# Four PSUM additions spread through the step of a graph attention, with a wait for each PSUM bank and a semaphore for the rescale

## The reference

```python
Q = (enh @ Wq + bq).reshape(N, H, D)
K = (enh @ Wk + bk).reshape(N, H, D)
V = (enh @ Wv + bv).reshape(N, H, D)
mod_k = K[src] + 0.2 * rel[:, None, :]
scores = jnp.einsum('ehd,ehd->eh', Q[dst], mod_k) / D ** 0.5
seg_max = jax.ops.segment_max(scores, dst, num_segments=N)
ex = jnp.exp(scores - seg_max[dst])
denom = jax.ops.segment_sum(ex, dst, num_segments=N)
w = ex / denom[dst]
agg = jax.ops.segment_sum(w[:, :, None] * V[src], dst, num_segments=N)
```

## Time and profile before

| | |
|---|---|
| median of 3 runs | 4579.15 us (4568.29 to 4586.91) |
| the profiled execution's own time | 4569.27 us |
| its span in the trace | 4567.5 us |
| busy over the span | PE 64%, DVE 57%, POOL 33%, ACT 26% |
| attention stage in the trace | first `modify` at 1051.1 us, last addition at 1880.2 us |
| DVE busy, in a stretch of 100 us of the middle of that stage | 84.8 to 89.1 us |
| PE busy, in the same | 69.5 to 75.1 us |

### The profile page before, as it was taken

The page is one execution under the profiler, slowest core; times in us unless marked ns, Lnnn a source line. Parts: engine busy times, 40 slices in busy tenths (PEclk is TensorE's granted clock), DMA queues, the critical chain, the costliest instruction groups (busy, mean ns, idle before and its releaser), DMA issues. The chain is left out here.

```text
span 4567.5 us, 54034 instructions
## 1 busy us (share of the span) xinstructions
PE 2922.7 (64%) x12877; PEld 1992.2 (44%) x12878; DVE 2614.3 (57%) x5653; ACT 1173.5 (26%) x4381; POOL 1510.3 (33%) x1422
## 2 busy tenths in 40 slices
PE   5555553254777777332095388988888628899980
PEld 4344442143444554122074244444444326677650
DVE  7766663346888888254812178788878830022221
ACT  0000000001555555201021044344444312233320
POOL 0377776005555554000000134344334305011114
PEclk9999999986778777565598689899889859999995
DMA  0000004315665665110000233333333307111112
GB/s 28 2 4 4 4 4 15 79 52 186 177 179 170 179 179 132 55 35 14 20 0 3 74 89 103 90 95 98 96 88 101 84 28 141 44 32 33 33 36 74
DMA packets 236997, 326.44 MB, mean 71 GB/s; under 512 B 115196, under 2 KB 166816, under 8 KB 236633
## 3 DMA queue, kind: packets, MB, share of 16 engines
q0 software_dynamic: 84512, 224.41, 19.0%
q1 hardware_dynamic: 117971, 95.44, 7.8%
q10 hardware_dynamic: 34402, 5.30, 1.0%
HBM read 291.54 MB, written 32.86 MB: 71 GB/s over the span
## 5 line engine op out<-in xcount | busy, mean ns | idle before, releaser
L1257 POOL DMA_INDIRECT g_rows<-h_d,g_idx x432 | 415.0, 961 | 1418.5 <-ACT g_idx L1272 1311.9
L925 POOL DMA_INDIRECT a_strip<-kv_d,src x416 | 433.5, 1042 | 593.3 <-POOLq L74 262.4
L484 POOL DMA_INDIRECT rec_d<-rec_s,place x400 | 476.2, 1190 | 243.9 <-issue 218.6
L949 ACT ACTIVATE x<-a_strip,x 128x64 f32<-128x64 f32 x1664 | 411.0, 339 | 223.9 <-PE a_psv L994 209.2
L994 PE MATMUL a_psv<-x 128*125 128x260 f32 x832 | 309.3, 507 | 157.8 <-DVE agg L1088 125.2
L384 PE MATMUL ps_base<-start,lo_hot_t 125*125 125x25 f32 x800 | 184.8, 384 | 264.0 <-DVE picked L439 263.3
L1350 PE MATMUL g_psa<-g_msg,g_hot 128*125 128x256 f32 x832 | 280.3, 468 | 110.3 <-DVE g_msg L1443 110.3
L384 PEld LDWEIGHTS ps_base<-start,lo_hot_t 125*125 125x125 f32 x800 | 175.5, 326 | 341.1 <-issue 339.6
L1338 PE MATMUL g_pso<-w_o,g_ut 128*128 128x256 f32 x840 | 294.0, 432 | 4.5 <-ACT g_lk L1280 4.5
L1350 PEld LDWEIGHTS g_psa<-g_msg,g_hot 128*125 128x125 f32 x832 | 161.8, 215 | 272.2 <-issue 169.6
L994 PEld LDWEIGHTS a_psv<-x 128*125 128x125 f32 x832 | 180.0, 240 | 222.6 <-DVE agg L1088 120.4
(11 more groups left out here) (374 smaller groups left out, 5722.1 us busy)
## 6 DMA issues: line engine op xcount, KB each, us to landing
a_row<-rows_d SPq DMA_DIRECT2D x104, 256.0 KB
e_w<-in_L_ffn_W1p SPq DMA_DIRECT2D x8, 1024.0 KB
e_w<-in_L_ffn_W2p SPq DMA_DIRECT2D x8, 1024.0 KB
y_d<-e_y SPq DMA_DIRECT2D x56, 128.0 KB, 1.7
g_rows<-h_d,g_idx POOLq DMA_INDIRECT x432
a_strip<-kv_d,src POOLq DMA_INDIRECT x416
rec_d<-rec_s,place POOLq DMA_INDIRECT x400
x<-in_x SPq DMA_DIRECT2D x2, 3125.0 KB
```

What stands on the lines that cost most here:

```text
L484: pool.indirect_dma_start(out=m.rec_d[:, :], out_offset=bass.IndirectOffsetOnAxis(ap=place[b][:, u:u + 1], axis=0), in_=rec_s[b][:, u, :], ...
L925: pool.indirect_dma_start(out=strip[:, lane.start + u, place:place + 2, :].rearrange("p a d -> p (a d)"), out_offset=None, in_=m.kv_d[:, : ...
L949: act.activation(msg[b][:, u, h, 0:HD], strip[:, lane.start + u, place, h * HD:(h + 1) * HD], ACT.Copy, scale=w[:, k * U + u, h:h + 1])
L1257: pool.indirect_dma_start(out=rows[r][:, u, 64:512], out_offset=None, in_=m.h_d[:, :], in_offset=bass.IndirectOffsetOnAxis(ap=idx[r][:, u: ...
```

## The change

It has four parts. The four additions, which stood in two pairs, are put one by one between the large DVE instructions: after `make`, after `modify`, after `multiply` and after `total`. `one_hot` moves from behind `total` to a place between the second addition and `multiply`. Each matmul of `aggregate` waits for the addition that last read its own bank, instead of both for all additions ahead. The rescale counts on a semaphore `s_scaled`, for which only DVE's next addition waits, and it moves with the register load to the head of the iteration.

```diff
         def added(s, u):
-            return 1 + s * U + u + s // CS
+            return 1 + s * U + u
...
                 if half == 0:
                     pe.wait_ge(s_hot, s + 1)
                     pe.wait_ge(s_wv, s + 1)
-                pe.wait_ge(s_add, added(s, 2 * half))
                 for u in (2 * half, 2 * half + 1):
+                    pe.wait_ge(s_add, added(s, u) - 1)
                     pe.matmul(ps_v[u % 2][:, 0:H * HW], hot[b][:, u, :],
...
+            def add(s, u, tiles):
+                if s < 0:
+                    return
+                dve.wait_ge(s_mm, s * U + u + 1)
+                dve.wait_ge(s_add, added(s, u))
+                if u == 0 and s >= CS and s % CS == 0:
+                    dve.wait_ge(s_scaled, s // CS)
+                agg = m.agg[:, tiles[u], :, :].rearrange("p h d -> p (h d)")
+                dve.tensor_tensor(agg, agg, ps_v[u % 2][:, 0:H * HW], ALU.add).then_inc(s_add, 1)
...
                 linked = 0 <= c < NC
+                tiles = node_tiles(v, ENGINE.DVE) if v >= 0 else None
+                if v > 0 and v % CS == 0:
+                    rescale(v // CS)
                 if now + 2 < STEPS:
                     make(now + 2)
                 if k == 0 and linked:
                     in_tile(c)
                 if k == 1 and linked:
                     raise_top(c)
+                add(v, 0, tiles)
                 if now < STEPS:
                     modify(now)
+                add(v, 1, tiles)
+                if 0 <= now - LAG < STEPS:
+                    one_hot(now - LAG)
+                if now < STEPS:
                     multiply(now)
-                if v >= 0 and v % CS == 0 and v:
-                    rescale(v // CS)
-                if v >= 0:
-                    tiles = node_tiles(v, ENGINE.DVE)
-                    add(v, (0, 1), tiles)
                 if k == 0 and linked:
                     across(c)
+                add(v, 2, tiles)
                 if now < STEPS:
                     total(now)
...
-                if 0 <= now - LAG < STEPS:
-                    one_hot(now - LAG)
-                if v >= 0:
-                    add(v, (2, 3), tiles)
+                add(v, 3, tiles)
```

More of the change, by code:

```diff
@@ L893, in build_attention @@
         s_add = sem("a_add")
+        s_scaled = sem("a_scaled")
         s_link = sem("a_link")
@@ L1094, in rescale @@
                 dve.wait_ge(s_fac, c + 1)
-                dve.wait_ge(s_add, added(c * CS, 0) - 1)
+                dve.wait_ge(s_add, added(c * CS, 0))
                 dve.tensor_tensor(m.agg[:, j, :, :], m.agg[:, j, :, :], fac[:, :, None].to_broadcast([P, H, HW]),
-                                  ALU.mult).then_inc(s_add, 1)
+                                  ALU.mult).then_inc(s_scaled, 1)
             def chain(c, n):
```

## The result

The changed kernel takes 4653.2 us (median of 4 runs, 4637.95 to 4670.31), the kernel before 4573.72 in the same comparison: ratio 1.0159, 95% interval 1.0126 to 1.0192. It is slower, and slower than the predicted 4590 and its range. In a later comparison, beside 23 runs of the kernel before, the same code came to 1.0097 (1.0071 to 1.0123); the part of the difference that I can't explain is told at e9.

The account below looks back on a forecast made before the run. DVE was taken to set the pace, TensorE having about two microseconds of slack per step at 2.4 GHz. Chunks +26, ordinary steps ahead -1, last steps -14 gave +11 us: median 4590 from 4579.15, range 4540 to 4640.

Parts of the forecast that it names:

- The ordinary step: Attention-stage step without link or rescale: 5.9 us at 2.4 GHz, 8.2 at 1.2, mean 6.3, against 6.51 before.
- the link step: Step with `across` and `spread_carry`: third addition waits 1.8 to 2.9 us for TensorE; 11.3 to 14.0 us, taken as 13.9.
- the rescale step: Step with the rescale: costs DVE 0.6 us more than an ordinary one, no longer makes TensorE wait, 6.9 us.
- The step ahead of the link: First addition needs `gather_ends`, with `modify` no longer between: 8.1 us at 2.4 GHz, 9.6 at 1.2, taken as 8.9.
- the one behind it: The step after the link step in each chunk, costed at 6.5 us.
- The last steps: Steps with no scores left: a wait per bank makes ScalarE the bound, 4.15 us for 5.51, -14 us in all.
- The spacing of the additions: On DVE, 118 waits between neighbouring additions (25.3 us) vanish when spread; DVE's own step falls 0.75 to 5.76 us.
- the rival by which the pause isn't the additions' wait: Spreading wins no pause on DVE; ordinary steps stay at 6.5 us, +13 more, 4603; chance 0.08.
- The register load: On DVE's sequencer, runs under `total` and costs nothing; without cover at most 0.3 us per step.
- The clock stays up: Rival: denser steps keep TensorE at 2.4 GHz through the link step; chunk 55.5 us, total -56, 4523; chance 0.20.
- The clock stays as low: Rival: half of ordinary time at 1.2 GHz, as now or lower; step 6.9 us, total +40, 4630; chance 0.25.
- my own case: The main forecast of 4590, with its own range of 4565 to 4610; chance 0.47.

Follow-up runs that it names:

- e9: The changed kernel run once more, unedited, in a later comparison; ratio 1.0097 to the kernel before.
- e1: The kernel before with only the new waits (one per PSUM bank, rescale on its own semaphore), DVE's old order kept; ratio 0.9925 to the kernel before.
- e7: The changed kernel with the third addition moved behind `total` and `pick` in link steps only; ratio 1.0031 to the kernel before.
- e8: The changed kernel with addition 0 between `modify` and `multiply`, the others behind `multiply`, `total` and `one_hot`, rescale behind `modify`; ratio 0.9779 to the kernel before.
- e12: The kernel before, its old waits kept, with additions and rescale placed late: addition 0 behind `modify`, others behind `multiply`, `total`, `one_hot`; ratio 0.9906 to the kernel before.
- e3: The changed kernel with `queries` reading fixed tiles, so TensorE loads no register and its matmuls use none; ratio 1.0054 to the kernel before.

## Why the prediction was wrong

**The ordinary step is the step that failed, by the price of the low clock in it.** The prediction named the right loop (addition 0, `modify`, addition 1, `one_hot`, `multiply`, `queries`, tile 0, addition 0) and gave it 5.9 us at 2.4 GHz and a mean of 6.3. It measured 7.40 in the profile after and 6.78 in e9. In parts, by e9:
- At 2.4 GHz: DVE's half is 3.62, as predicted (3.63); the way back is 2.46 for 2.28, and the step 6.08 to 6.27. `queries` after an idle stretch take 1.50, not the 1.4 read off rows in which they followed other matmuls, and the handing over 0.14, not 0.06.
- The clock: I took 22% of the time at 1.2 GHz. In e9's four ordinary steps the granted clock is 0.87, which is 25%, so the share was nearly right. The price wasn't. I had priced low time by the whole-step loop through `relations` and tiles 2 and 3 (8.2), as if it fell evenly. By those two values a step with a granted clock of 0.77, 46% of it low, would take 6.8 us. These steps took 7.2 to 7.6, since the low time fell on `queries` and tile 0, the one stretch for which DVE waits, and went into the short loop in full.
- That makes 6.3 into 6.8, 2 us per chunk. The other 0.6 us of the profile after is the late addition 0 that e9 didn't repeat, and a lower clock in ordinary steps (0.82).

The ordinary steps were to pay for the link step, and they paid nothing: the four and the rescale step together were to take 32.1 us. They took 33.6 in e9, and in e1, with the old order, 33.2.

The step ahead of the link (9.6 to 9.9 for 8.9) and the one behind it (6.6 to 7.3 for 6.5) were priced too near their values at 2.4 GHz: in e9 the granted clock of the step ahead is 0.67, where the kernel before had 0.80. By e9 the terms miss 3.4 us per chunk, 37 us in 11, and 11 + 37 = 48 is what e9 measured above its kernel before (4582.37 - 4533.1 = 49). The closeness owes something to luck, as the kernel before has no profile from that comparison and its chunk of 59.0 is the first profile's. The other 30 of the first comparison's 80 us go with the late addition (2.9 us per chunk), whose cause stays open.

**What was right.** The link step: 13.9 predicted, 13.8 measured, with the pause of 2.8 us at the predicted place, and e7 took 2.2 us of it out by giving back the cover. The last steps: ScalarE the bound at 3.9 us (4.15 predicted), 16 us gained for 14. The spacing of the additions: 25.3 us of waits fell to 3.4, and e8's 5.71 us show DVE's sum of 5.76 to be right, so the rival by which the pause isn't the additions' wait is out. (The section of the Trainium skill, "VectorE: DVE Perf Modes", "The DRAIN you can't avoid", on which that rival leans says itself that an instruction that is not held starts earlier; the prediction left this out.) The register load was free: no pause of e8 or e9 belongs to it. The rescale holds TensorE no longer, and e12 against e8 shows that this is worth up to 2.1 us per chunk.

**The rivals.** "The clock stays up" is out; the granted clock of ten chunks is 0.79 in the profile after and in e9, as it was in the middle of the stage before. "The clock stays as low" had the right sign and, by e9, nearly the right time (4630 for 4579 is 1.011). Its reason held: the loops are rigid, and what TensorE loses at 1.2 GHz DVE can't make up. Its condition didn't: it wanted half of the ordinary time at 1.2 GHz for a step of 6.9, and 25% was enough for 6.8. So its number is partly luck. I gave it 0.25 and my own case 0.47, since I expected the denser steps to raise the clock. In ordinary steps it did rise against the first profile, from 0.79 to 0.82 and, in e9, 0.87, but not by the order and not by denser work: e1, with the old order, has 0.90 there, and TensorE was busy 73% of these steps before, 70% in the profile after, 72% in e9 and 76% in e1. A step that waits in a loop isn't denser. Over the ten chunks e1 has 0.85 and e9 0.79, so with the same waits the new order lowers the clock, in the link step (0.70 to 0.62) and ahead of it (0.85 to 0.67) above all:

```profile
1132.41:1706.85 574.44, 432.37 (x2661) 274.49 (x2660) 522.82 (x911) 327.62 (x1382) 332.53 (x320) 0.85 0.62 184
1133.02:1780.98 647.96, 451.73 (x2661) 302.63 (x2660) 508.06 (x911) 327.44 (x1380) 306.94 (x320) 0.79 0.55 163
```

The first line is e1's, the second e9's.

## What to carry to other kernels

Before an instruction is spread into gaps of a busy engine, trace the loop through the other engine: each operation put between the one that receives a result and the one that releases the next sits in the period, even if it fills a gap (here `modify`, 1.21 us, and `one_hot`, 0.67; taking one of them out of the loop gave 1.3% and 1.1%). Put the receiving instruction as late as its own successor allows and the releasing one directly behind it; then spreading gains (e8, 2.2%). And judge each part of a change alone: here a gain of 0.75% by finer waits was hidden behind a loss by order, and with the right order the same waits were worth 0.9% by the traces and 1.3% by the ratios of two comparisons.

## What the runs showed of the hardware

- The granted clock alternates from step to step in a loop of 6 to 7.6 us: 0.77 and 1.00 in turn in e9's ordinary steps, with TensorE 69 to 75% busy. The engine pauses 1.32 us (1.47 in one step) ahead of `relations` and 0.55 ahead of `queries`; the fall comes in that second pause or as `queries` start (at 1242.03 in the step above, `queries` at 1242.05; at most 0.5 us ahead of them and 0.15 behind their start). In e8, at 77% busy, it is 0.90 over ten chunks.
- Twelve `queries` matmuls with an address from a register take 1.50 us, at times up to 1.66, to the start of the next group after an idle stretch at 2.4 GHz, and 1.31 with fixed addresses (e3).
- One and the same program showed 0.82 us in one profile and 1.57 in another between a matmul's start and the addition that it releases, in rows that are otherwise equal; the count came late, not the addition behind it. The four runs of the one comparison were slower than the six of the other, so a whole comparison can carry such an offset: the unedited kernel belongs among the experiments, early.
